# Interleaving the tail of one 512-token block with the projections and the head of the next, in the Q/K/V stage of a two-layer kernel on eight cores

## The reference

```python
def poincare_fully_connected(x, z, r, c):        # c = 1
    lam = 2.0 / (1.0 - c * jnp.sum(x * x, axis=-1, keepdims=True))
    z_norm = jnp.maximum(jnp.linalg.norm(z, axis=0), EPS)
    two_cr = 2.0 * c_sqrt * r
    inner = x @ (z / z_norm)
    v = 2.0 * z_norm / c_sqrt * jnp.arcsinh(c_sqrt * lam * inner * jnp.cosh(two_cr)
                                            - (lam - 1.0) * jnp.sinh(two_cr))
    w = jnp.sinh(c_sqrt * v) / c_sqrt
    return w / (1.0 + jnp.sqrt(1.0 + c * jnp.sum(w * w, axis=-1, keepdims=True)))

xn = layernorm(x)
Q = poincare(xn, z_q, b_q);  K = poincare(xn, z_k, b_k);  V = xn @ w_v.T + b_v
x = x + layernorm(softmax_attention(Q, K, V, 16 heads))
x = x + layernorm(rwkv_style_ffn(layernorm(x)))
```

## Time and profile before

| what | us |
|---|---|
| median of the 2 timed runs | 3498.52 (3493.33 and 3503.71) |
| the profiled execution, slowest core | 3498.34 |
| its span in the trace (core 6) | 3496.8 |
| spans of the other cores | 3475.9 to 3495.4 |
| busy: TensorE / VectorE / ScalarE | 1849.0 / 1454.1 / 1683.7 |
| Q/K/V stage of sequence 0, from its first projection to the end of its last tail | 142.95 to about 690 |
| Q/K/V stage of sequence 1, likewise | 1850 to about 2392 |

### The profile page before, as it was taken

How to read it: one execution, slowest core, us unless ns; L and a number is a source line. 1 busy time by engine, 2 the same in 40 slices (tenths; PEclk the granted TensorE clock), 3 DMA queues, 4 the chain that set the end, 5 groups by cost and what they waited for, 6 DMA issues and landing times.

```text
span 3496.8 us, 27938 instructions; the slowest of 8 cores (3475.9 to 3496.8 us)
## 1 busy us (share of the span) xinstructions
PE 1849.0 (53%) x7343; PEld 574.9 (16%) x7360; DVE 1454.1 (42%) x2455; ACT 1683.7 (48%) x1721; POOL 162.3 (5%) x256
## 2 busy tenths in 40 slices
PE   0352352057777687681506352422776877867504
PEld 0120121011122121120202120110111211212101
DVE  2344444301443644626424544441116355364363
ACT  0225534457756747651102535542776476565501
POOL 0000011100000000000000010011000000000000
PEclk9975786578889898896757685766888988989857
DMA  5421111262222404311062121017223133141211
GB/s 80 104 61 30 43 37 35 47 120 66 75 57 61 118 16 104 91 26 49 14 130 59 39 61 28 21 37 137 66 62 84 38 94 77 40 114 41 56 31 37
DMA packets 325787, 217.11 MB, mean 62 GB/s; under 512 B 276224, under 2 KB 284544, under 8 KB 325632
## 3 DMA queue, kind: packets, MB, share of 16 engines
q1 hardware_dynamic: 287488, 109.87, 14.2%
q0 software_dynamic: 38144, 105.45, 12.3%
HBM read 169.03 MB, written 42.21 MB: 60 GB/s over the span
## 4 chain that ended last, share of the span: by engine, by line
ACT 29%; DVE 24%; PE 24%; DMA 10%; issue 7%; SPq 3%; DVEq 1%; POOL 1%; ACTq 1%; another core or an unknown queue 0%; POOLq 0%
ACT pool L1036 16%; PE psc L608 3%; PE psc L880 3%; DVE pool L804 3%; PE psc L860 3%; PE p_attA L980 2%; DMA pool<-x 2%; PE psc L647 2%; DVE dump L371 2%; DVE dump L368 2%; DMA pool<-s_vaug 2%; PE psc L1011 2%; ACT pool L496 2%; PE p_attB L988 2%; ACT pool L499 2%
## 5 line engine op out<-in xcount | busy, mean ns | idle before, releaser
L1036 ACT ACTIVATE pool<-psc 128x1024 bf16<-128x1024 f32 x1024 | 1047.9, 1023 | 574.7 <-PE psc L1018 497.5
L980 PE MATMUL p_attA<-pool 128*65 128x512 bf16 x1024 | 434.7, 425 | 392.2 <-ACT pool L1036 200.2
L1011 PE MATMUL psc<-pool 64*128 64x512 bf16 x1024 | 423.0, 423 | 92.5 <-DMA pool<-s_vaug 92.5
L988 PE MATMUL p_attB<-pool 128*65 128x512 bf16 x1024 | 433.2, 423 | 0.0
L1018 PE MATMUL psc<-pool 64*128 64x512 bf16 x1024 | 423.2, 423 | 0.0
L1041 DVE CAST pool<-p_attA 1x512 bf16<-1x512 f32 x64 | 43.8, 685 | 825.0 <-PE p_attB L988 804.2
L542 PE MATMUL psc<-pool,ones_bf 128*128 128x512 bf16 x126 | 55.4, 619 | 448.1 <-DVE pool L534 448.1
L839 PE MATMUL psc<-pool,w_sb 128*128 128x512 bf16 x512 | 133.9, 421 | 245.3 <-DVE smc L827 237.6
L980 PEld LDWEIGHTS p_attA<-pool 128*65 128x65 bf16 x1024 | 115.1, 112 | 720.2 <-issue 720.2
L454 PE MATMUL psc<-dump,ones_bf 128*128 128x512 bf16 x57 | 32.0, 586 | 360.3 <-DVE dump L448 360.3
L1011 PEld LDWEIGHTS psc<-pool 64*128 64x128 bf16 x1024 | 91.4, 94 | 561.2 <-issue 561.2
(11 more groups left out here) (128 smaller groups left out, 2404.5 us busy)
## 6 DMA issues: line engine op xcount, KB each, us to landing
pool<-s_vaug SPq DMA_DIRECT2D x64, 520.0 KB, 4.9
pool<-s_kfm SPq DMA_DIRECT2D x64, 512.0 KB, 3.4
pool<-x POOLq DMA_DIRECT2D x8, 2048.0 KB, 8.7
pool<-x POOLq DMA_DIRECT2D x32, 512.0 KB, 3.8
out<-pool POOLq DMA_DIRECT2D x32, 512.0 KB, 2.9
s_vaug<-pool POOLq DMA_DIRECT2D x32, 260.0 KB, 2.3
s_qfm<-pool POOLq DMA_DIRECT2D x32, 256.0 KB, 4.4
s_kfm<-pool POOLq DMA_DIRECT2D x32, 256.0 KB, 4.6
```

Source lines behind the costliest of these rows:

```text
L980: T(lambda t, c=c, po=po, vof=vof: t.matmul(p_attA[0:65, :], vsl[:, vof:vof + 65], PT[:, po:po + 512], start=(c == 0), stop=(c == 15), ski ...
L988: tk = T(lambda t, c=c, po=po, vof=vof: t.matmul(p_attB[0:65, :], vsl[:, vof + 65:vof + 130], PT[:, po + 512:po + 1024], start=(c == 0), s ...
L1011: T(lambda t, kof=kof, qof=qof, reg=reg: t.matmul(psc[:, reg:reg + 512], Ksl[0:64, kof:kof + 128], Qsl[0:64, qof:qof + QB], start=True, st ...
L1036: lambda s, reg=reg, po=po: s.activation(PT[:, po:po + 1024], psc[:, reg:reg + 1024], AF.Exp, scale=0.125),
```

## The change

The arithmetic, the tiles and the buffers stay the same. `emit_head` is cut in two behind its transposes: `emit_head1` (load, statistics, normalization, transposes) and `emit_head2` (squares, matmuls with ones, `lam_b`). `emit_tails` is cut into eight pieces: `s1` (L492), `s23` (L496, L499), `s4` (L503), `s5` (L507), `s6` (L511), `s78` (L517, L520, L523) and `fin` (L534 to L581). The value projection is called in two halves, tiles 0 and 1 and tiles 2 and 3. In a block the pieces are called in a new order. Block 0 and the tail after the loop come out in the order that they had. The core of the diff:

```diff
-            for which, wslot in [("q", 0), ("k", 1)]:
+            def emit_proj(which, wslot, ...):      # the same body
...
-            if qb + 1 < NQB:
-                hd = emit_head(qb + 1)
-            if bnd_p is not None:
-                emit_tails(bnd_p)
-            for tt in range(4):
+            def emit_vproj(tts, ...):
+                for tt in tts:                     # the same body
...
+            st = tails_mk(bnd_p) if bnd_p is not None else None
+            emit_proj("q", 0)
+            if st:
+                tails_s1(st)
+            emit_proj("k", 1)
+            if st:
+                tails_s23(st)
+                tails_s4(st)
+            hd1 = emit_head1(qb + 1) if qb + 1 < NQB else None
+            if st:
+                tails_s5(st)
+                tails_s6(st)
+            if hd1 is not None:
+                hd = emit_head2(hd1)
+            if st:
+                tails_s78(st)
             pc["hev"] = [hev_bank[12], hev_bank[13], hev_bank[14],
                          hev_bank[15]]
+            emit_vproj((0, 1))
+            if st:
+                tails_fin(st)
+            emit_vproj((2, 3))
```

More of the change, by code:

```diff
@@ L433, in emit_head @@
                     waits=[tk_ln, pc.get("xtm_free_%d" % par)], inc=1))
-            pass
+            tS_ln = p.last["s"]
             tk_xf = []
@@ L444, in emit_head, with emit_head2 @@
             pc["xtm_free_%d" % par] = tk_xf_all
+            return {"xf_all": tk_xf_all, "par": par, "base": base,
+                    "xnf": xnf, "tk_xn3": tk_xn[3], "tS_ln": tS_ln}
+        def emit_head2(hd):
+            par = hd["par"]
+            xnf = hd["xnf"]
+            lamb = lam_b2[par]
+            tk_xf_all = hd["xf_all"]
             tk_x2c = [None] * NCH
@@ L471, in emit_head, with tails_mk @@
                 waits=[tks], inc=1)
[L472 to L479, removed]
+            pc["x_cons"] = [hd["tk_xn3"], hd["tS_ln"], tk_lmm[NCH - 1]]
+            hd["lam"] = tk_lam
+            return hd
+        def emit_head(qb):
+            return emit_head2(emit_head1(qb))
+        def tails_mk(bnd):
             HB = NCH * QB // 2
@@ L488, in emit_tails, with tails_s1 @@
                         "tz": "tzq" if which == "q" else "tzk",
-                        "tk": hev_toks[wi * NCH + h * 4 + 3],
+                        "tk": bnd["hev"][wi * NCH + h * 4 + 3],
                     })
-            for un in units:
+            return {"bnd": bnd, "units": units}
+        def tails_s1(st):
+            for un in st["units"]:
                 un["tk"] = V(lambda v, un=un: v.tensor_mul(
@@ L494, in emit_tails, with tails_s23 @@
                     waits=[un["tk"], pc["bh_free"][un["u"]]], inc=1)
-            for un in units:
+        def tails_s23(st):
+            for un in st["units"]:
                 Sc(lambda s, un=un: s.activation(
@@ L501, in emit_tails, with tails_s4 @@
                     inc=1)
-            for un in units:
+        def tails_s4(st):
+            for un in st["units"]:
                 un["tk"] = V(lambda v, un=un: v.tensor_add(
@@ L505, in emit_tails, with tails_s5, tails_s6 @@
                     waits=[un["tk"]], inc=1)
-            for un in units:
+        def tails_s5(st):
+            for un in st["units"]:
                 un["tk"] = Sc(lambda s, un=un: s.activation(
                     un["Ah"], un["Ah"], AF.Ln), waits=[un["tk"]], inc=1)
-            for un in units:
+        def tails_s6(st):
+            for un in st["units"]:
                 for dc in range(un["h"] * 4, un["h"] * 4 + 4):
@@ L515, in emit_tails, with tails_s78 @@
                         waits=[un["tk"]], inc=1)
-            for un in units:
+        def tails_s78(st):
+            for un in st["units"]:
                 Sc(lambda s, un=un: s.activation(Bh4[un["u"]][:],
@@ L598, in build_nc, with emit_proj @@
             hev_bank = {}
-            for which, wslot in [("q", 0), ("k", 1)]:
+            def emit_proj(which, wslot, par=par, xnf=xnf, lamb=lamb,
+                          tk_xf_all=tk_xf_all, tk_lam=tk_lam):
                 cq, sq = (("cqq", "sqq") if which == "q"
@@ L635, in build_nc, with emit_vproj @@
                         smcol(sq, dc), None, ALU.add), inc=1)
+            def emit_vproj(tts, qb=qb, xnf=xnf, tk_xf_all=tk_xf_all):
+                for tt in tts:
+                    tk_vp = [None, None]
+                    for hf in range(2):
+                        for ci in range(NCH):
+                            tk_vp[hf] = T(lambda t, tt=tt, hf=hf, ci=ci,
+                                          xnf=xnf: t.matmul(
+                                p_v[hf],
+                                xnf[:, tt * D + ci * 128:
+                                    tt * D + (ci + 1) * 128],
+                                w_slot(2, ci, hf * 512, (hf + 1) * 512),
+                                start=(ci == 0), stop=(ci == NCH - 1),
+                                skip_group_check=True),
+                                waits=[tk_xf_all, tk_vst_dma[tt % 2],
+                                       pc["vev"][hf]],
+                                inc=(1 if ci == NCH - 1 else 0))
+                    vst = v_st[:, (tt % 2) * NH * 65:
+                               (tt % 2 + 1) * NH * 65].rearrange(
+                        "p (h x) -> p h x", x=65)
+                    for hf in range(2):
+                        pc["vev"][hf] = V(lambda v, hf=hf, vst=vst:
+                                          v.tensor_tensor(
+                            vst[:, hf * 8:(hf + 1) * 8, 0:64],
+                            p_v[hf].rearrange("p (h x) -> p h x", x=64),
+                            bv_row[:, hf * 512:(hf + 1) * 512].rearrange(
+                                "p (h x) -> p h x", x=64), ALU.add),
+                            waits=[tk_vp[hf], tk_bv], inc=1)
+                    tk_pk = V(lambda v, vst=vst: v.tensor_copy(
+                        vst[:, :, 64:65], ones_bf[:, 0:16].unsqueeze(2)),
+                        waits=[tk_ones], inc=1)
+                    tk_vst_dma[tt % 2] = G(
+                        lambda g, tt=tt, qb=qb: g.dma_start(
+                            out=s_vaug[qb * 4 + tt, :, :],
+                            in_=v_st[:, (tt % 2) * NH * 65:
+                                     (tt % 2 + 1) * NH * 65]),
+                        waits=[tk_pk], inc=16, sem="g_vst%d" % (tt % 2))
```

19 lines of the change are left out of this document (16 added, 3 removed).

## The result

The changed kernel took 3444.18 us (median of 9 runs) against 3499.4 us for the kernel before (8 runs). The ratio is 0.985, with a 95% interval of 0.983 to 0.987: 1.5% less. The forecast was 3444 us.

A forecast was written before the change was run, and what follows sets the result against it. The prediction held that the order of the work, not an engine, bounds six blocks. Savings of 41.4 us in four full blocks and 12.6 in block 3 sum to 54.0: 3498.3 - 54.0 = 3444 us, range 3427 to 3466.

The forecast's parts named there:

- Value tiles 0 and 1: First half of the value projection, now ahead of `fin`: 7.32 us behind `s78`, with TensorE's tile 0 hidden.
- Tiles 2 and 3: Second half of the value projection, behind `fin`: repeats the pattern of tiles 0 and 1, 6.15 us to the block's end.
- The row of 5.30 us: Earlier trace row of 15 recorded value matmuls, cold in its first eight; the forecast used it twice per block.
- The full blocks and block 3: Savings: 41.4 us in four blocks with head and tail; 12.6 us in two runs of block 3, which has no head.
- The clock of TensorE: Whether value matmuls behind waits run at half or full speed; left undecided, with savings between 34 and 83 us.
- the middle: Forecast's choice on TensorE's clock: value patterns partly at half speed, saving 54 us, 3444 us; chance 0.72.
- the cold case: Both value patterns at half speed throughout: 1.7 us more each time, 20 us in all, leaving a saving of 34 us.
- warm end: Both value patterns at full speed, first sums of `fin` gaining up to 1.5 us in six blocks: 83 us saved together.
- Rival A: Value tiles 1 and 3 stay at half speed on TensorE: 3464 us, a saving of 34; chance 0.10.
- Rival B: More than order: full-speed TensorE, 3415 us; second, one attention load moves by 17 us either way, 3427 or 3461; chance 0.13.
- Rival C: Transposes come late and delay the second head part, `s78` and all behind: slower, 3554 us at 30 us late; chance 0.02.
- Rival D: Order changes but time doesn't, the tail's ScalarE work having been covered elsewhere: blocks keep 140 us, 3498 us; chance 0.03.

The follow-up runs named there:

- e8_warm_tensor: Changed kernel plus extra matmuls of ones, never read, in TensorE's idle time ahead of value tile 1 in blocks 1 to 3; ratio 0.982 to the kernel before.
- e4_value_split_only: Kernel before, in its old order, with only the value projection cut in two around `fin`; ratio 0.993 to the kernel before.
- e1_squares_back: Changed kernel with the four squares `s1` moved back from between the Q and K groups to behind the K groups; ratio 0.990 to the kernel before.
- e3_head_whole: Changed kernel with the next block's head in one piece again, ahead of `s5`; ratio 0.990 to the kernel before.
- e9_roots_first_only: Order of e4_value_split_only, but with `s1`, `s23` and `s4` behind the K groups, ahead of a head in one piece; ratio 0.995 to the kernel before.

## Why the prediction was right, point by point

**What bounds the kernel.** That the blocks are held by the order of the work stands: the kernels of the table, `e8_warm_tensor` aside, do the same work in a full block, and it lasts from 140.0 down to 99.3 us.

**The layout of block 2.** The forecast against the rows of block 2 above, on the block's clock (0 at 341.38):

| step | forecast | measured |
|---|---|---|
| first `s23` | 28.93 | 28.65 |
| last `s4` ends | 46.6 | 46.3 |
| head1 ends | 58.0 | 57.7 |
| `s6` ends | 65.2 | 65.1 |
| ScalarE's `s78` begins | 73.4 | 73.35 |
| VectorE gets to the value tiles | 91.2 | 91.1 |
| `fin` begins | 98.5 | 99.2 |
| tiles 2 and 3 begin | 123.6 | 124.0 |
| block ends | 129.7 | 129.8 |

It was right because durations of the same instruction did not change with what ran beside it (`s5` 7.92 us, head1 11.28, in both kernels), so that only the order had to be worked out. Two terms were off by more than 0.3 us, in opposite directions. *Value tiles 0 and 1* took 8.10 us instead of 7.32, since tile 1 took 5.98 us for 16 matmuls, not the 5.30 of the earlier trace rows. *Tiles 2 and 3* took 5.74 instead of 6.15 (4.90 us for tile 3 in the last row of TensorE), and `fin` 24.81 instead of 25.02. So the block's end is met to 0.1 us in part because errors cancelled; the four full blocks lasted 128.4 to 130.8 us. The row of 5.30 us was not typical either: in the kernel before, tile 1 took 5.25 and 5.30 us in two of the six blocks and 5.98 to 6.07 in the other four. One number of the working is wrong without a consequence: ScalarE's part of the tail begins not 26 but 27.4 us earlier by the forecast's own rows (56.37 to 28.93), and 27.7 as measured.

**The full blocks and block 3.** Forecast savings of 11.1, 10.6, 9.0 and 10.7; measured 10.0, 10.5, 10.3 and 10.7: 41.4 forecast, 41.4 measured. Block 3: 109.7 forecast, 110.96 and 110.99 measured. Both its patterns of tiles 1 and 3 ran long (5.91 and 6.58 us for 16 matmuls, in the chain of the first sequence). So the mis-sized term is block 3, 12.6 forecast and 10.0 measured. The sum, 54.0, was 51.4 in the blocks of this core and 48.9 to 52.0 in those of the other three of its die, while their whole spans became 47.5 to 48.4 us shorter. The 6.9 us elsewhere on core 6 were in no step of mine and stay unexplained. That the median time moved by 55 us, as forecast to 1 us, is therefore partly luck.

**The clock of TensorE.** The choice of the middle was a little too good: tiles 1 and 3 of the six blocks took 68.7 us together, where twelve times 5.30 is 63.6, so a quarter of the 20 us to the cold case was lost. What the runs add is the price: keeping TensorE busy through the wait is worth 15.7 us in six blocks, 2.4 us at each tile 1, where the text had taken 1.7. Its warm end, 83 us with both patterns and the sums at full speed, was not reached even with the extra matmuls.

**The batches.** By the Trainium skill's sentence on matmuls in batches ("Perfetto Trace Analysis", section Matmul Optimizations), the saving should have been, as I had worked it out, the 34 us of the cold case. It was 51.4 us in the blocks, and `e4_value_split_only`, the cut alone, gains 22 to 27 of them. The batch of this kernel was already broken by a wait for stores (3.51 us in the earlier trace rows).

**Rival A** came by a quarter at most, as the 68.7 us show. **Rival B's** second mechanism was no mechanism. The load that ends the wait at the start of the second attention stage took 45.69 us after the change and 28.30 before, and I had priced the difference at 17 us. The waits in the first 100 us or so of that stage (who waited for whom, total, times, longest), and a window of it, of the changed kernel, and then of the kernel before:

```profile
PE psc L1068 <- DMA pool<-s_vaug: 47.0, 2, 38.3
...
2338.84:2450.00 111.16, 60.90 (x236) 14.32 (x236) 8.21 (x12) 60.12 (x59) 5.25 (x8) 0.77 0.60 120
```

```profile
PE psc L1011 <- DMA pool<-s_vaug: 45.0, 1, 45.0
...
2392.85:2504.01 111.16, 61.54 (x240) 14.63 (x240) 8.21 (x12) 61.28 (x60) 5.25 (x8) 0.77 0.60 120
```

TensorE waited 47.0 us for such loads in one and 45.0 in the other, and got through 236 and 240 matmuls. The two rows belong to different loads. In the second sequence before, the chain names the first load. After the change, and in the first sequence before it (two waits, 47.5 us), TensorE had begun on the first load, and the chain names the second, which it waited for 8.7 us more after the change. The chain names the load that came last, and that load's own duration is not what it costs. **Rival C** did not come; nothing waits in front of L455, so the transposes landed in time. **Rival D** is excluded by the blocks.

## What to carry to other kernels

Where engines take turns, lay one period out by hand, instruction by instruction, with durations from the trace. It gave the mean full block to 0.1 us (the single ones to 1.3) and showed the next gap: the idle time on ScalarE that the forecast named was 10.5 us, and moving three operations took 11.7 us off each full block. Large operations can be put into the gaps of an engine that empties PSUM, one by one, as long as its sum stays near that of the matmuls and the banks give some slack. An interleaving has to be judged whole: one of its moves was worth nothing alone, and another needs it.

## What the runs showed of the hardware that I had not expected

Behind the same 2.65 us without a matmul TensorE went on at 2.4 GHz in some blocks and at half that in others, within one kernel. The changed kernel shows 3.36 us for the eight sums in block 2 above, and full speed in block 1 of the second sequence:

```profile
1984.50 5.24 PE L681 MATMUL psc<-w_sb,pool 128*128 128x512 bf16 x16 [15.59 <-DVE pool L696]
1992.39 1.02 PE L568 MATMUL psc<-pool,ones_bf 128*128 128x512 bf16 x4 [2.65 <-DVE pool L560]
1993.72 1.02 PE L568 MATMUL psc<-pool,ones_bf 128*128 128x512 bf16 x4 [0.30 <-DVE pool L560]
```

In `e8_warm_tensor` it is half and half, although tile 1 had run at full speed each time. So the length of an idle gap of that size did not tell which level follows. What did go with it was how tile 1 had run: in the 24 blocks of the changed kernel, `e1_squares_back`, `e3_head_whole` and `e4_value_split_only` (core 6), the first eight sums took 2.35 us in all 11 where tile 1 took 5.67 us or less, and 3.25 to 3.57 us in all 13 where it took 5.73 us or more, that is, where the clock had risen late or hardly at all. Over all the cores that the table names for these kernels and `e9_roots_first_only`, 168 blocks, three fall outside that border. That is an observation of these runs; its cause was not tested, and in `e8_warm_tensor` it does not hold.

Of the same kind are the last blocks with the same program, 109.4 and 111.0 us: the 16 matmuls of tile 3 took 4.9 us in one and 6.6 in the other, behind waits of 4.45 and 4.52 us.

ScalarE's evacuations took 0.78 us each with activations of 2 us between them as without, and four PSUM banks absorbed a delay of 2 us on each second group with no visible gap on TensorE.
